# Turning gathered token rows on TensorE and ScalarE instead of with transposing DMAs

## The reference

```python
q_top, q_idx = top_k(einsum('bnd,gd->bgn', x, w_qr), 512)     # per sequence b and group g
queries      = x[bidx, q_idx]
kv_top, kv_idx = top_k(einsum('bnd,gd->bgn', x, w_kvr), 256)
key_values   = x[bidx, kv_idx]
q    = einsum('bgnd,ged->bgne', queries, w_q)
k, v = split(einsum('bgnd,ged->bgne', key_values, w_kv))      # 8 heads of 64
v    = v * sigmoid(kv_top); one null key and value per head is put in front
o    = softmax(q k^T / 8) v;  o = (o w_out) * sigmoid(q_top)
out[token] = mean of the o rows routed to it, or null_token where there is none
```

## Time and profile before

| | |
|---|---|
| median of 3 runs | 3709.2 us |
| the profiled execution | 3700.87 us, its span 3699.5 us |
| mean granted PE clock | 0.977 of full speed |
| busy over the span | PE 94%, DVE 81%, ACT 66%, POOL 50% |
| DMA, mean and queue of plain DMAs | 93 GB/s; 29.2% of 16 engines' time |
| chain that ended last | PE 62%, DVE 12%, issue 4%, ACT 4%, DMA 2%, POOL 2% |

### The profile page before, as it was taken

One profiled execution on the slowest core, in us unless ns is written; L12 is line 12 of the kernel. 1 busy time (PEld: TensorE's weight loads), 2 busy tenths in 40 slices (PEclk: granted clock), 3 DMA queues, 4 the chain that ended last, 5 costly groups with the idle time before them and its releaser, 6 DMA issues.

```text
span 3699.5 us, 69323 instructions
## 1 busy us (share of the span) xinstructions
PE 3483.2 (94%) x26872; PEld 2087.5 (56%) x26872; DVE 2988.8 (81%) x5336; ACT 2438.0 (66%) x4585; POOL 1856.1 (50%) x1483
## 2 busy tenths in 40 slices
PE   7899999999999999999857999999999999999998
PEld 4555555565555555555533555555665565566655
DVE  6898888989889889898977777778777877877774
ACT  6777677676767777776625665667665766566665
POOL 1332333323333333332425888878666766666666
PEclk9899999999999999999967999999999999999999
DMA  4233323233223333322448466577556656665553
GB/s 146 61 88 82 82 55 77 78 80 90 67 68 73 85 78 81 78 55 67 80 46 168 93 116 110 99 116 155 103 103 106 141 106 107 114 113 103 106 104 43
DMA packets 500407, 344.42 MB, mean 93 GB/s; under 512 B 241415, under 2 KB 424839, under 8 KB 498032
## 3 DMA queue, kind: packets, MB, share of 16 engines
q1 hardware_dynamic: 443760, 237.06, 29.2%
q0 software_dynamic: 56320, 102.94, 16.3%
HBM read 176.19 MB, written 101.71 MB: 75 GB/s over the span
## 4 chain that ended last, share of the span: by engine, by line
PE 62%; DVE 12%; issue 4%; ACT 4%; DMA 2%; POOL 2%; SPq 0%; another core or an unknown queue 0%; ACTq 0%; DVEq 0%; POOLq 0%
PE pair L1366 7%; PE pair L1481 7%; PE pair L1327 6%; PE pair L1241 6%; PE pair L1289 5%; PE pair L1381 4%; PE pair L1395 4%; PE pair L1337 3%; PE pair L1442 2%; PE pair L1441 2%; PE pair L1411 2%; DVE cv L1631 2%; PE pair L1462 2%; PE pair L1460 1%; PE pair L1461 1%
## 5 line engine op out<-in xcount | busy, mean ns | idle before, releaser
L2313 POOL TENSOR_TENSOR ph<-pf,ph 128x512 f16<-128x512 f32 x256 | 362.4, 1416 | 279.7 <-ACT ph L2176 277.6
L1631 DVE SCALAR_TENSOR_TENSOR cv<-raw,taps,cv 128x512 f32<-128x512 f32 x480 | 418.1, 893 | 20.6 <-ACT cv L2043 18.9
L1884 DVE TENSOR_REDUCE smx<-pair 128x2 f32<-128x514 f32 x512 | 350.9, 686 | 54.2 <-PE pair L1411 50.9
L1241 PE MATMUL pair<-xhT,whi 128*128 128x512 f16 x1280 | 381.4, 380 | 5.8 <-DVE dts L1589 5.7
L1289 PE MATMUL pair<-zhi,xhT 128*128 128x512 f16 x1024 | 331.1, 385 | 14.4 <-DVE yb L1709 10.7
L2170 ACT ACTIVATE pf<-pair 128x1024 f32<-128x1024 f32 x256 | 261.9, 1023 | 110.8 <-PE pair L1442 97.3
L1919 DVE TENSOR_TENSOR ph<-pf,ph 128x512 f16<-128x512 f32 x256 | 240.3, 939 | 100.0 <-ACT ph L2176 96.4
L1327 PE MATMUL pair<-ohi,yT 128*128 128x512 f16 x1024 | 318.9, 383 | 1.2 <-ACT yT L2101 1.1
L2073 ACT ACTIVATE de<-de,cum 128x128 f32<-128x128 f32 x1024 | 311.2, 388 | 1.1
L2176 ACT CAST ph<-pf 128x1024 f16<-128x1024 f32 x256 | 267.5, 1045 | 5.8
L2318 POOL TENSOR_TENSOR ohl<-of,ohl 128x256 f16<-128x256 f32 x256 | 222.5, 870 | 75.0 <-ACT ohl L2181 73.7
(11 more groups left out here) (269 smaller groups left out, 10185.0 us busy)
## 6 DMA issues: line engine op xcount, KB each, us to landing
de<-cum SPq DMA_DIRECT2D x64, 1024.0 KB, 9.5
rows<-rowt SPq DMA_DIRECT2D x16, 1040.0 KB, 4.2
xin<-x SPq DMA_DIRECT2D x16, 1024.0 KB, 13.6
y<-xin SPq DMA_DIRECT2D x16, 1024.0 KB, 4.3
y<-ob POOLq DMA_DIRECT2D x64, 256.0 KB, 4.4
qb<-qa SPq DMA_DIRECT2D x32, 512.0 KB
rbc<-rank SPq DMA_DIRECT2D x63, 256.0 KB
wst<-wkv SPq DMA_DIRECT2D x32, 256.0 KB
```

Source lines behind the costliest of these rows:

```text
L1241: ins = pe.matmul(bk[:], w[:, k, ws], xt[:, ha, k, :], start=n == 0, stop=n == 3 * KD - 1)
L1631: ve.scalar_tensor_tensor(c_[:], r_[:, t:t + BLK], taps[:, ct, t:t + 1], c_[:], ALU.mult, ALU.add).then_inc(done, 1)
L1884: ve.tensor_reduce(smx[:, qt, 2 * h2:2 * h2 + 2], sc[:, :, 0:NK + 1], AX.X, ALU.max)
L2313: po.tensor_tensor(p_[:, 1, 1], f[:, 1], p_[:, 0, 1], ALU.subtract).then_inc(S.plp, 1)
```

## The change

`row` is no longer a DMA. PE transposes the gathered tile: eight 128x128 float16 transposes, against the float16 identity, into one PSUM bank; a new ACT step `row_out` copies the bank into `xq` or `xk` as 512 float32 words per partition. The dependencies follow: `q` waits for four `row_out` (semaphore `xr`), `k` and `v` for six, `gather` of the next item waits only until PE has read the same tile. PE's line gets six more steps for each item: those of item 0 and 1 ahead of the heads, those of item n+2 woven into item n by the new `Part`; two other parts (`maxima`, `finish`) get slightly other shares. In the listing the DVE step `row_score` goes with the name `row_out`.

```diff
+    "row": [("single", 1, 1.2)],                        # USES: one bank
+    "row": [(0.6, "row_out")],                          # THEN
+    "row": lambda n, j: (("gather", n, j), 4.0),        # AFTER
...
-        add("SP", ROW_ISSUE, ("row", 0, j), [("gather", 0, j), ("z", NCH - 1, 1)], extra=ROW_LANDS)
+        add("ACT", 0.6, ("row_out", 0, j), [("row", 0, j), ("z", NCH - 1, 1)])
...
-                add("SP", ROW_ISSUE, ("row", n, j), [("gather", n, j), read], extra=ROW_LANDS)
+                add("ACT", 0.6, ("row_out", n, j), [("row", n, j), ("q", n - 1, KD - 1) if j < QT else ("v_low", n - 1, KT - 1)])
...
-            others.append(Part(Feed(maxima(n + 1), 10.2, record), -0.5, 1.1))
+            others.append(Part(Feed(maxima(n + 1), 10.2, record), -0.6, 1.1))
-            others.append(Part(Feed(finish(n - 1), 10.4, record), -0.8, 1.1))
+            others.append(Part(Feed(finish(n - 1), 10.4, record), -1.0, 1.0))
+        if n + 2 < ITEMS:
+            others.append(Part(Feed(turn_rows(n + 2), RT * 0.43, record), -1.9, 1.25))
...
+            def row(n, j):                               # on PE
+                g16 = gat[j][:].bitcast(F16)
+                q.wait_ge(S.gat[j], 16 * (n + 1))
+                wait_given_back(q, "row", n, j)
+                b16 = bank("row", n, j)[:].bitcast(F16)
+                for c in range(2 * KD):
+                    ins = pe.transpose(b16[:, c * P:(c + 1) * P], g16[:, c * P:(c + 1) * P], id16[:])
+                ins.then_inc(S.gt_mm, 1)
...
+            def row(n, j):                               # on ACT
+                q.wait_ge(S.gt_mm, RT * n + j + 1)
...
+                ac.copy(dst[:].bitcast(F32)[:, :, s0 * P // 2:(s0 + 1) * P // 2],
+                        bank("row", n, j)[:].rearrange("p (c t) -> p c t", c=2 * KD)).then_inc(S.xr, 1)
...
             def gather(n, j):
-                q.wait_ge(S.xr[j // QT], 16 * (KT if j // QT else QT) * n)
+                q.wait_ge(S.gt_mm, RT * (n - 1) + j + 1)
...
-                sp.dma_start_transpose(dst[:, :, s0 * P:(s0 + 1) * P], gat[j][:].bitcast(F16)[:, 0:2 * D]).then_inc(S.xr[j // QT], 16)
```

More of the change, by code:

```diff
@@ L49 @@
 NSLOT = 4
-ROW_ISSUE, ROW_LANDS = 0.6, 4.0
 NW = 4 * D
@@ L441, in arrange @@
     alone = Order(plan.twin(), first, ahead=AHEAD_M)
-    arrange_steps(alone, [step for step in line if step[0] not in ("rank_in", "slots")], False)
+    arrange_steps(alone, [step for step in line if step[0] not in ("rank_in", "slots", "row")], False)
     alone.run()
@@ L493, in arrange_steps @@
             add("PE", 0.5, step, [("ranks", len(RANKS) - 1)], [("single", [("taken",)])])
+        elif name == "row":
+            add("PE", 0.45, step, [("gather", 0, b)], [("single", [("row_out", 0, b)])])
         elif name == "intra":
@@ L622, in arrange_items @@
     for j in range(RT):
-        done += [(name, 0, j) for name in ("rank", "gather", "row")]
-        if j >= QT:
-            done.append(("row_score", 0, j))
+        done += [(name, 0, j) for name in ("rank", "gather", "row", "row_out")]
     order = Order(plan, done, keep=KEEP, ahead=AHEAD)
@@ L650, in arrange_items @@
         name, n, k = (*step, 0)[:3]
-        if name in "qkv":
-            after = each("row", n, QT if name == "q" else RT) + [("weight_low", n // NB, NSP // 4 * ("qkv".index(name) + 1) - 1)]
+        if name == "row":
+            after = [("gather", n, k)]
+        elif name in "qkv":
+            after = each("row_out", n, QT if name == "q" else RT) + [("weight_low", n // NB, NSP // 4 * ("qkv".index(name) + 1) - 1)]
         elif name == "max":
@@ L686, in arrange_items @@
             for j in range(RT):
[L687 to L691 removed]
+                add("POOL", 1.05, ("gather", n, j), [("slot", n), ("row", n - 1, j), ("row_out", n - 1, j)], extra=4.0)
+                add("ACT", 0.6, ("row_out", n, j), [("row", n, j), ("q", n - 1, KD - 1) if j < QT else ("v_low", n - 1, KT - 1)])
         two = ("score", n - 2, H - 1)
@@ L699, in arrange_items @@
             add("DVE", 1.4, ("k_low", n, e), [("k_out", n, e)])
-            add("ACT", 0.7, ("v_out", n, e), [("v", n, e), ("row_score", n, RT - 1), ("value", n - 2, H - 1)])
+            add("ACT", 0.7, ("v_out", n, e), [("v", n, e), ("row_out", n, RT - 1), ("value", n - 2, H - 1)])
             add("DVE", 0.75, ("v_low", n, e), [("v_out", n, e)])
@@ L817, in make_plan @@
     record.append(("slots",))
+    for j in range(RT):
+        record.append(("row", 0, j))
     arrange(plan, record.steps)
@@ L820, in make_plan, with turn_rows @@
     plan.append(("mamba_done",))
+    def turn_rows(n):
+        for j in range(RT):
+            yield ("row", n, j)
+            yield 0.43
     def prepare(n):
@@ L871, in make_plan @@
     record = Record()
-    for gen in (prepare(0), maxima(0)):
+    for gen in (prepare(0), maxima(0), turn_rows(1)):
         Feed(gen, 1, record).to(1)
@@ L1147, in program @@
             "slots": lambda: [(S.topk, 5)],
+            "row": lambda n, j: [(S.xr, RT * n + j + 1)],
             "q": lambda n, e: [(S.qlo, KD * n + e + 1)],
```

52 lines of the change are left out of this document (24 added, 28 removed).

## The result

The changed kernel takes 3759.85 us (median of 4 runs, 3757.54 to 3766.13) against 3705.03 us before (4 runs, 3697.33 to 3711.38). The ratio is 1.0149, 95% interval 1.0132 to 1.0167: 55 us slower. A second measurement of the same kernel on another chip gave 1.0149 (1.0129 to 1.0170). The direction was as forecast; the forecast of 3805 us and its range from 3765 us were too high.

The account below looks back on a forecast made before the run. PE was taken to bound the second stage's items; 85.4 (PE steps) - 8 (start) + 18 (ACT copies) = 95.4 us, against a 3709.2 us median giving 3804.6, say 3805 us, range 3765 to 3850 us.

Parts of the forecast that it names:

- what goes: SP's 192 transposing DMA issues and their traffic disappear; given nothing beyond the start, as hidden beside PE.
- the start: Start of the second stage: item 0's `q` 3 us earlier plus 5 us for a rank load, together -8 us.
- ACT's copies: 192 new bank copies on ACT, 0.586 us each; one of six taken to show in an item, +18 us.
- What PE's steps cost: 192 new transposing steps on PE, 0.445 us each at full clock, adding 85.4 us.
- What bounds the kernel: In the second stage's items PE is the bound, busy 96 to 98% from 1997 us on; DVE next at 78%.
- the rival of a falling clock: PE's clock falls to the 1.2 GHz level around the transposes: +288 us, 3997 us; chance 2%.
- 0, at most 3 either way: First stage: only neighbouring steps near its end exchange places, worth 0, at most 3 us either way.
- The 5 us for the load of ranks: At the start, SP's load of item 1's ranks no longer stands behind the transposing DMAs: 5 us taken of 8.1.
- The 10.8 us of issue waits ahead of scores: PE's waits ahead of scores, following DMAs into `qb`; the most that removing the transposing DMAs could give, 10.8 us.
- the gap-filling rival: New PE steps fall into PE's idle gaps after 1997 us: only +38 us, 3747 us; chance 7%.
- the ACT rival: ACT and PSUM banks become the limit in an item's second half: +138 us, 3848 us; chance 11%.
- The rival "not slower": Transposing DMAs delay everything, and removing them gives back at least 74 us of PE's idle time: 3690 us; chance 4%.

Follow-up runs that it names:

- e3_pe_twice: The changed kernel with every tile's eight PE transposes done twice into the same bank, no more copies; ratio 1.0321 to the kernel before, +119 us.
- e5_ranks_first: The kernel before with SP's load of item 1's ranks issued ahead of item 0's six transposing DMAs; ratio 0.9997.
- e9_no_rows: The kernel before without the transposing DMAs of items 1 to 31 and the waits for them; ratio 0.9950, -18.5 us.
- e13_hybrid: The kernel before with PE transposes and ACT copies for item 0's tiles only, later items keeping their DMAs; ratio 0.9969, -11.5 us.
- e6_pe_only: The kernel before, DMAs kept, with PE also transposing every tile of items 1 to 31 into a bank nobody reads; ratio 1.0240, +89 us.
- e10_no_copies: The changed kernel without ACT's copies of items 1 to 31 and the waits for them; ratio 1.0134 to the kernel before, changed kernel beside it 1.0149.
- e12_table_late: The kernel before with the early order of the first stage's tail and the score table's store issued after item 0's transposing DMAs; ratio 1.0009.

## Why the prediction was wrong, step by step

Three terms of the sum failed: what goes (0, measured -18.5 us), the start (-8, measured about -21 with some 6 us of the former in it) and ACT's copies (+18, measured +6 to +9). What PE's steps cost was right.

**What bounds the kernel, and PE's 192 steps: right.** PE's busy time rose by 87.3 us for 85.4 forecast; a step takes 0.445 us in the changed kernel; the fourteen items hold 758.97 - 721.94 = 37.0 us more PE work for 14 x 2.67 = 37.4. The granted clock of the item stretches stayed at 1.00, so the rival of a falling clock found nothing: 16 transposes in a row still start 56 ns apart. The Trainium skill ("TensorE: Matmul & The Clock Gate", Part 4: PE-mode transpose) says that the clock gate does not count transposes as it counts products. No run here tests that, since all the transposes of the items stand among products; with double sets (e3_pe_twice) the clock is 1.00 as well. One reading of the prediction was off: PE is busy 96 to 98% in the two long stretches only, and 133.70 / 147.00 = 91% in the last.

**The start: mis-sized, and its reason wrong.** Forecast -8 us with a bound of -20. The two profiles give -21.1 us at item 2, with the steps of the first items in it. Of its parts, the order of the first stage's tail was set to "0, at most 3 either way" and is worth -10.7 us. That was the largest error within the start: I compared the orders only around the new steps, while a due time had run back through the gathers and ranks to the top-k bits. `q` of item 0 follows the table's store after 21.7 to 24.7 us in the seven executions that turn item 0 on PE, and after 25.7 to 27.4 in the six with DMAs: about 4 us, for which I had 3. The 5 us for the load of ranks were nothing (e5_ranks_first). In their place items 1 and 2 came about 6 us earlier with their own DMAs gone: item 0 to item 2 takes 101.8 us before, 95.7 in e9_no_rows; and 98.1 in e13_hybrid, 92.2 in the changed kernel. Why the last is shorter still, with new steps of PE in it, is open; e6_pe_only, with such steps and the DMAs, takes 101.4 us, so these steps cost nothing there. The prediction also put most of PE's first wait of 23.14 us down to the gather: the gather's tile was taken only once the table's store had landed.

**ACT: +18 us forecast, about +6 to +9 measured** (e10_no_copies). The step that failed is the guess that one copy of six shows through. Waits for a copy are there, 7.3 us of them, at the banks, but the kernel without the copies is only 6 to 9 us faster.

**What goes: 0 forecast, -18.5 us measured** (e9_no_rows), some 6 of them the ones at items 1 and 2 just told. I argued that no row of PE's waits names SP or a transposing DMA, and took absence of a name for absence of a cost. The 10.8 us of issue waits ahead of scores, which I named as the most it could give, are 1.4 us in the changed kernel, but that is not the DMAs' doing alone. With the DMAs gone and PE's old order (e9_no_rows) they are 4.6 us, with the DMAs kept and the new order (e6_pe_only) 1.9.

The terms as measured: 85.4 (PE) - 10.7 (order) - 4 (item 0 turned sooner) - 18.5 (DMAs gone) + 6 to 9 (copies) = 58 to 61 us, for 55 measured. The pieces were taken on different chips, with intervals of 6 to 8 us either way, and need not add up exactly. The changed shares of the other parts (`maxima`, `finish`) were never timed by themselves; in e6_pe_only they come with PE's steps. The expectation of 56.2 us for the period was 55.26; with 54 for the gap-filling rival and 57.5 for the ACT rival, neither was the case. The rival "not slower" was right that the DMAs stand in the way, at a quarter of the size that it needed; that it is SP's queue was not shown.

## What to carry to other kernels

When a step gets a follower or loses one in a planned order, compare the whole order of every engine and not the place of the edit: here a due time moved the end of the other stage and was worth about 11 us in a change that cost 55. Price a transfer that "runs beside" the bound engine by leaving it out, since what it delays shows up under the names of others; and price an added copy by how long it holds the buffer that the bound engine wants next, not by the load of its own engine.

## What the runs showed of the hardware

- A gather issued behind the store of the score table (128 KB of 16-byte pieces, landing after 15.3 to 18.7 us) was first taken 6.8 to 12.8 us after its own issue, and never before the store had landed (thirteen executions); with the store moved behind, 3.5 us (e12_table_late).
- Copying a bank a second time cost 0.28 us of the kernel's time per 0.59 us copy (53 us / 192), the first 0.03 to 0.05 us. The same instruction differed in price by a factor of five or more.
- Eight float16 transposes of 128x128 cost 0.445 us in a full stream, and a second eight in the same place 0.33 us more (64 us / 192). PE's idle time fell from 14.7 to 5.8 us in fourteen items meanwhile.
- 192 transposing DMAs that PE's list of waits names twice cost 18.5 us (e9_no_rows).
